# Opening pass of a language-model tower: stacked queries and keys straight from the projection, remainders subtracted on TensorE

## The reference, cut to what matters

```python
left = jnp.einsum('bad,dr->bar', x, W1)         # W1: 128 x 10, "queries"
right = jnp.einsum('rd,bcd->brc', W2, x)        # W2: 10 x 128, "keys"
scores = jnp.einsum('bar,brc->bac', left, right)
attn = jax.nn.softmax(scores / sqrt(512), axis=-1)
out = jnp.einsum('bac,bcd->bad', attn, x)
```

## Time and profile before

| what | us |
| --- | --- |
| median of 3 timed runs | 1693.22 (1692.04 to 1693.26) |
| the profiled execution, its own time | 1697.35 |
| its span, first to last instruction | 1695.5 |
| opening pass, until the second pass's first matmul | 138.9 |
| second pass with the router | 138.9 to about 256 |

### The profile page before, as it was taken

How to read it: one execution, slowest core, us unless ns; L and a number is a source line. 1 busy time by engine, 2 the same in 40 slices (tenths; PEclk the granted TensorE clock), 3 DMA queues, 4 the chain that set the end, 5 groups by cost and what they waited for, 6 DMA issues and landing times. The chain is left out here.

```text
span 1695.5 us, 37358 instructions
## 1 busy us (share of the span) xinstructions
PE 1521.0 (90%) x8662; PEld 660.5 (39%) x8662; DVE 1242.6 (73%) x3454; ACT 1102.5 (65%) x2137; POOL 1018.9 (60%) x1375
## 2 busy tenths in 40 slices
PE   2767975889999999999999999999999999875998
PEld 0215962233333333333333333333333333212665
DVE  4995866478787878878787887878788887353442
ACT  1432770647878777787877878787777878823333
POOL 6841435466685677767567677757767775423443
PEclk9767986879999999999999999999999999957999
DMA  1321117365454565456456546546645643020221
GB/s 41 77 54 31 45 32 108 50 81 72 70 83 67 70 75 84 62 74 81 61 75 77 77 60 83 75 60 81 77 72 65 85 63 55 10 30 29 62 67 56
DMA packets 134645, 109.27 MB, mean 64 GB/s; under 512 B 24128, under 2 KB 127552, under 8 KB 134592
## 3 DMA queue, kind: packets, MB, share of 16 engines
q1 hardware_dynamic: 132544, 104.45, 41.9%
q0 software_dynamic: 2048, 4.20, 1.0%
HBM read 19.26 MB, written 8.39 MB: 16 GB/s over the span
## 5 line engine op out<-in xcount | busy, mean ns | idle before, releaser
L1122 ACT ACTIVATE probs<-psum 128x512 f32<-128x512 f32 (+3 forms) x1536 | 757.9, 550 | 256.2 <-PE psum L1237 247.4
L1022 DVE TENSOR_REDUCE mx_S<-psum 128x1 f32<-128x512 f32 x512 | 324.7, 679 | 50.3 <-PE psum L1217 50.0
L1022 DVE TENSOR_REDUCE mx_C<-psum 128x1 f32<-128x512 f32 x512 | 316.3, 676 | 32.0 <-PE psum L1217 32.0
L1018 DVE CUSTOM_DVE_ANT_0 psum<-psum,causal 128x128 f32<-128x128 f32 (+3 forms) x512 | 241.4, 515 | 95.3 <-PE psum L1217 94.2
L1217 PE MATMUL psum<-ks_S,qs_S 96*128 96x512 bf16 x512 | 197.0, 395 | 17.9 <-DVE mx_S L1022 8.7
L1217 PE MATMUL psum<-ks_C,qs_C 96*128 96x512 bf16 x512 | 199.8, 398 | 12.2 <-DVE mx_C L1022 9.5
L1237 PE MATMUL psum<-qs_C,ks_C 99*128 99x512 bf16 x512 | 188.6, 387 | 3.3 <-ACT probs L1122 2.9
L1237 PE MATMUL psum<-qs_S,ks_S 99*128 99x512 bf16 x512 | 188.0, 384 | 0.2 <-ACT probs L1122 0.2
L903 POOL CAST parts_q<-f_q 128x512 bf16<-128x512 f32 x48 | 29.2, 609 | 251.1 <-ACT f_q L1113 250.6
L1217 PE MATMUL psum<-ks_T,qs_T 96*128 96x128 bf16 (+3 forms) x512 | 157.4, 310 | 5.1 <-DVE mx_T L1018 3.7
L1237 PE MATMUL psum<-qs_T,ks_T 99*128 99x256 bf16 (+3 forms) x512 | 152.3, 302 | 1.8 <-ACT probs L1122 1.7
(11 more groups left out here) (182 smaller groups left out, 2720.1 us busy)
## 6 DMA issues: line engine op xcount, KB each, us to landing
qs_S<-parts_q SPq DMA_DIRECT2D x96, 128.0 KB, 4.4
ks_S<-parts_k SPq DMA_DIRECT2D x96, 128.0 KB, 4.8
qs_T<-parts_q SPq DMA_DIRECT2D x96, 128.0 KB, 4.5
ks_T<-parts_k SPq DMA_DIRECT2D x96, 128.0 KB, 4.6
qs_C<-parts_q SPq DMA_DIRECT2D x96, 128.0 KB, 4.4
ks_C<-parts_k SPq DMA_DIRECT2D x96, 128.0 KB, 4.8
w_in_S<-in_s_in SPq DMA_DIRECT2D x16, 257.0 KB, 2.8
w_in_T<-in_t_in SPq DMA_DIRECT2D x16, 257.0 KB, 2.7
```

The lines of the kernel that those rows point to most:

```text
L1018: nc.vector.tensor_tensor_reduce(tile[:, 0:last_key], tile[:, 0:last_key], causal[:, T - last_key:T], 1.0, NEG, ALU.add, ALU.max, mx[kind] ...
L1022: nc.vector.tensor_reduce(mx[kind][:, n:n + 1], tile, AX_X, ALU.max, negate=True).then_inc(reduced, 1)
L1122: nc.scalar.activation(probs[:, group_place(kind, b, n // 4), n % 4, t0:T], psum[:, LOGITS + ring_place(kind, b, n, RC), t0:T], ACT.Exp, s ...
```

## The change

The projection's weights are widened from 64 to 128 columns on the host: the 10 query columns stand six times in columns 0 to 59 and the 10 key columns six times in 64 to 123. The projection so writes all six groups of queries to partitions 0 to 59 of a PSUM bank and of keys to 64 to 123. The parts are peeled off inside the bank. ACT rounds the whole bank to bf16 (`part[0]`), and PE adds `minus[:, 0, :]` times that to the bank, where `minus` is a diagonal of -1 in those columns whose group wants a later part. The same is done with `part[1]` and `minus[:, 1, :]`. After it each group of the bank holds what its part is a rounding of, and one rounding copy by ACT (queries) and one by DVE (keys) fills 64 partitions of `qsd` and `ksd`. No part passes through SBUF copies by SP any more, and POOL and DVE make none. In the same diff:
- two banks take turns for the projection; lags shrink to 1, 2 and 3 batches; PE and DVE have two pairs of straight code;
- the normalisation moves from DVE to ACT as scale and shift (`shift` is new on DVE);
- `X` is filled by one transfer of SP for each batch instead of an ACT copy;
- POOL starts to gather when the ids are in, and no longer waits for the other six loads;
- the second pass's first logits wait for all reductions, and `negate(1)` is waited for only ahead of the first mix;
- the matmuls of scores and logits contract over 64 and 67 partitions instead of 96 and 99.

The core of the diff:

```diff
-                def stack(pair):
-                    at_least(sp, stacked, 16 * 2 * NPROD * pair)
-                    sp.wait_ge(lr_lo, 2 * pair + 2)
-                    both = bass.ds(2 * pair, 2)
-                    for g in range(NPROD):
-                        sp.dma_start(qsd[HD * g:HD * g + HD, both, :], parts[0:HD, Q_PARTS[g], both, :])\
...
+                def keep(b, odd):
+                    sp.wait_ge(normed1, b + 1)
+                    sp.dma_start(X[:, bass.ds(NB * b, NB), 0:P], xs[:, odd, :, :]).then_inc(x_kept[odd], 16)
...
-                pool.wait_ge(loaded, 16 * LOADS)
+                pool.wait_ge(ids_in, 16)
...
                 nc.vector.memset(X[:, :, P:P + 1], 1.0)
-                nc.vector.memset(ksd[RA:RA + 32, :, :], 1.0)
+                nc.vector.memset(minus[:], 0.0).then_inc(minus_set, 1)
                 dve.wait_ge(consts, 2)
+                dve.wait_ge(minus_set, 1)
+                for k, columns in enumerate(LATER):
+                    for a, e in columns:
+                        last = nc.vector.tensor_scalar(minus[:, k, a:e], ident[:, a:e], -1.0, None, ALU.mult)
+                last.then_inc(minus_set, 1)
+                nc.vector.memset(ksd[RA1:RA1 + 32, :, :], 1.0)
...
# DVE, first_norm(b, odd), after the statistics of batch b
+                    for k in range(2):
+                        if exists(b - SCORE_LAG):
+                            c = b - SCORE_LAG
+                            dve.wait_ge(scored, 2 * c + k + 1)
+                            nc.vector.tensor_reduce(mx[:, bass.ds(NB * c + 2 * k, 2)],
                                                     psum[:, 2 * k:2 * k + 2, :], AX_X, ALU.max).then_inc(reduced, 1)
+                        if k == 0 and exists(b):
+                            dve.wait_ge(std1, b + 1)
...
+                            nc.vector.scalar_tensor_tensor(out=shift[:, odd, :], in0=mv[:, :, 0], scalar=-1.0,
+                                                           in1=rstd[:, odd, :], op0=ALU.mult, op1=ALU.mult)\
+                                .then_inc(shift1, 1)
+                        if k == 0 and exists(b - PART_LAG):
+                            c = b - PART_LAG
+                            dve.wait_ge(taken[1], c + 1)
+                            nc.vector.tensor_copy(ksd[0:RA1, bass.ds(c, 1), :].rearrange("p o t -> p (o t)"),
+                                                  psum[KEYS_AT:P, LR[odd], :]).then_inc(k_ready, 1)
...
# ACT, factors(b, odd), c = b - PART_LAG: in this order
+                        nc.scalar.activation(part[0][:], psum[:, LR[odd], :], ACT.Copy).then_inc(part_ready[0], 1)
+                        nc.scalar.activation(xT[:], psum[:, TURN, :], ACT.Copy).then_inc(xT_ready, 1)
                         nc.scalar.activation(std[:], mv[:, :, 1], ACT.Sqrt, bias=eps_t[:, 0:1]).then_inc(std1, 1)
+                        nc.scalar.activation(part[1][:], psum[:, LR[odd], :], ACT.Copy).then_inc(part_ready[1], 1)
...
+                        for n in range(NB):
+                            last = nc.scalar.activation(xs[:, odd, n, :], tokens(h, b, n), ACT.Identity,
+                                                        bias=shift[:, odd, n:n + 1], scale=rstd[:, odd, n:n + 1])
...
+                        nc.scalar.activation(qsd[0:RA1, bass.ds(c, 1), :].rearrange("p o t -> p (o t)"),
+                                             psum[0:RA1, LR[odd], :], ACT.Copy).then_inc(q_ready, 1)
...
+                def take(c, odd, k):
+                    pe.wait_ge(part_ready[k], c + 1)
+                    nc.tensor.matmul(psum[:, LR[odd], :], minus[:, k, :], part[k][:], start=False, stop=(k == 1),
+                                     skip_group_check=True).then_inc(taken[k], 1)
...
# PE, factors(b, odd), t, c, d = b - 1, b - 2, b - 3: four transposes of t, then
+                        scores(d, 0)
+                        take(c, odd, 0)
+                        nc.tensor.matmul(psum[:, LR[1 - odd], :], w12_t[:], xT[:], start=True, stop=False,
+                                         skip_group_check=True).then_inc(lr_ready, 1)
+                        take(c, odd, 1)
+                        scores(d, 1)
```

More of the change, by code:

```diff
@@ L26 @@
 RB = RA + NPART
+D1 = 10
+KEYS_AT = P // 2
+RA1 = P // 2
+RB1 = RA1 + NPART
 GQ = H // 4
@@ L201, in embed_and_mix @@
         xT = sb("xT", [P, T])
-        parts = sb("parts", [64, NPART, B, T], BF16)
+        part = [sb("part0", [P, T], BF16), sb("part1", [P, T], BF16)]
+        minus = sb("minus", [P, 2, P], BF16)
         qsd = sb("qsd", [P, B, T], BF16)
@@ L269, in _ @@
                 sp.dma_start(norm_cols[:], norms).then_inc(loaded, 16)
-                def stack(pair):
-                    at_least(sp, stacked, 16 * 2 * NPROD * pair)
-                    sp.wait_ge(lr_lo, 2 * pair + 2)
-                    both = bass.ds(2 * pair, 2)
-                    for g in range(NPROD):
-                        sp.dma_start(qsd[HD * g:HD * g + HD, both, :], parts[0:HD, Q_PARTS[g], both, :])\
[L278 to L284, removed]
+                def keep(b, odd):
+                    sp.wait_ge(normed1, b + 1)
+                    sp.dma_start(X[:, bass.ds(NB * b, NB), 0:P], xs[:, odd, :, :]).then_inc(x_kept[odd], 16)
+                halves_of_pairs(sp, keep, 1, B // 2, B // 2)
                 for half in range(2):
@@ L320, in fetch @@
                         ).then_inc(got[b % 2], 16)
[L322 to L331, removed]
+                for b in range(B):
+                    fetch(b)
                 def root(stats, var, done, number, mv, vare, rstd, used=None):
@@ L502, in factors @@
-                    if exists(b):
[L503 to L509, removed]
+                    if exists(c):
+                        act.wait_ge(taken[0], c + 1)
+                        at_least(act, taken[1], c)
+                        nc.scalar.activation(part[1][:], psum[:, LR[odd], :], ACT.Copy).then_inc(part_ready[1], 1)
@@ L558, in turn_maxima, with scores @@
                         .then_inc(max_turned, 1)
+                def scores(c, half):
+                    at_least(pe, reduced, 2 * c - 1 + half)
+                    for n in range(2 * half, 2 * half + 2):
+                        last = nc.tensor.matmul(
+                            psum[:, n, :], qsd[0:RA1, bass.ds(c, 1), P * n:P * n + P].rearrange("p o t -> p (o t)"),
+                            ksd[0:RA1, bass.ds(c, 1), :].rearrange("p o t -> p (o t)"), start=True, stop=True)
+                    last.then_inc(scored, 1)
+                def take(c, odd, k):
+                    pe.wait_ge(part_ready[k], c + 1)
+                    nc.tensor.matmul(psum[:, LR[odd], :], minus[:, k, :], part[k][:], start=False, stop=(k == 1),
+                                     skip_group_check=True).then_inc(taken[k], 1)
                 def factors(b, odd):
@@ L574, in factors @@
-                    if exists(b):
-                        pe.wait_ge(normed1, b + 1)
-                        at_least(pe, xT_ready, b)
-                        for n in range(NB):
-                            last = nc.tensor.transpose(psum[:, TURN, P * n:P * n + P], xs[:, odd, n, :], ident[:])
-                        last.then_inc(turned1, 1)
-                    if exists(b):
-                        pe.wait_ge(xT_ready, b + 1)
-                        at_least(pe, lr_rem, b)
-                        nc.tensor.matmul(psum[0:64, LR, :], w12_t[:], xT[:], start=True, stop=True).then_inc(lr_ready, 1)
@@ L1533, in thirds @@
         return w[0:P], w[P:2 * P], w[2 * P:3 * P]
-    w12 = np.zeros((P, 64), np.float32)
-    w12[:, 0:10] = a["attn_W1"]
-    w12[:, 32:42] = a["attn_W2"].T
+    w12 = np.zeros((P, P), np.float32)
+    for g in range(NPROD):
+        w12[:, D1 * g:D1 * g + D1] = a["attn_W1"]
+        w12[:, KEYS_AT + D1 * g:KEYS_AT + D1 * g + D1] = a["attn_W2"].T
     given = {
```

115 lines of the change are left out of this document (61 added, 54 removed).

## The result

The changed kernel takes **1702.32 us** (median of 18 runs, 1693.04 to 1707.49) against 1692.88 (median of 18, 1691.12 to 1693.76) for the kernel before in the same comparison: ratio 1.0053, 95% interval 1.0042 to 1.0064. That is slower by more than 0.2%. I had predicted 1668.3 and gave "slower" 0.04.

The account below looks back on a forecast made before the run. DVE and POOL were taken to fill the opening pass's steps. Starting the second pass at 114.0 instead of 138.9 saves 24.9 us: 1697.35 becomes 1672.4, less 4.1 gives 1668.3 us; range 1652 to 1682.

Parts of the forecast that it names:

- some other loss: Catch-all without a place or mechanism: an unnamed loss eats the gain; chance 0.04.
- The one about straight code and loops: Opening pass: loops entered at batch 4 cost two more 2.4 us stalls, PE at slower clock; 1680 us; chance 0.15.
- The gather's start: Opening pass on POOL: gather after the ids alone begins about 2.5 us sooner; first statistics near 10.9, 1.2 gained.
- The early idle stretches: Opening pass before batch 4: 10 us of idle stretches stay whole, so batch 4's statistics begin at 40.7.
- The rival in which the gather binds: Opening pass: steps catch up with POOL, first logits at 98 to 104, time 1652 to 1658; chance 0.20.
- The step: Opening pass, per batch from batch 4: 5.85 us at the slower clock, 4.8 at the faster, taken as 5.3.
- half and half: PE's clock in the opening pass: slower and faster level taken in equal parts, giving a 5.3 us step.
- The key copy: DVE's step in the opening pass: copying keys out of PSUM, 64 partitions by 512, taken as 0.65 us.
- The tail: Opening pass from batch 15's statistics to the last reduction: 14.5 us, then 0.5 to the first logits at 114.0.
- SP's maxima rows: End of opening pass: first half's maxima rows land before 114, within a microsecond or two of the first logits.
- Table loads: ACT's step in the opening pass: two 1.28 us loads between root and normalisation; step 8.4, time 1706; chance 0.03.
- the 4.1: Whole kernel: the profiled run lay 4.1 us above the timed median, so 1672.4 became 1668.3.

Follow-up runs that it names:

- experiment 3: The kernel before with 38 idle DVE instructions ahead of the second pass: 1728.92 us, median of three, ratio 1.0213.
- experiment 6: The changed kernel with 90 idle DVE instructions right ahead of the expert loop: 1667.93 us, ratio 0.9855.
- experiment 11: The changed kernel with four pairs of straight DVE code in the opening pass instead of two, no idle instructions: 1663.49 us, ratio 0.9826.
- experiment 7: The changed kernel with 90 idle DVE instructions ahead of the second pass, an earlier file run again on a third chip: 1664.62 us, ratio 0.9831.
- experiment 1: The changed kernel with 90 idle DVE instructions ahead of the second pass, first run: 1723.54 us, ratio 1.0161.
- experiment 2: The changed kernel with 128 idle DVE instructions ahead of the second pass: 1767.75 us, ratio 1.0403.
- experiment 4: The changed kernel with 97 idle instructions on ACT ahead of its expert loop, DVE's code not moved: 1760.61 us, ratio 1.0387.
- experiment 9: The changed kernel with 62 idle DVE instructions ahead of its expert loop: 1667.58 us, timed once.
- experiment 10: The changed kernel with 218 idle DVE instructions ahead of its expert loop: 1681.99 us, timed once.
- experiment 12: The changed kernel with four pairs of straight DVE code, and POOL waiting for all seven loads before gathering: 1667.87 us, ratio 0.9845.
- experiment 5: The changed kernel run again unchanged on another chip: 1697.29 us, ratio 1.0025.
- experiment 8: The changed kernel with 22 idle DVE instructions ahead of its expert loop: 1683.0 us, timed once.

## Why the prediction was wrong

By its own steps:

- **"The second pass behind it keeps its instructions, and so do the later stages. I carry the difference in the start of the second pass to the end without loss."** This is the step that failed. The instructions are the same, but not their places in DVE's stream. 33.75 us were gained up to the second pass and 42.3 us lost in the expert loop. Experiments 3 and 6 show both halves by themselves: the loss without the change, and the change without the loss. My rivals had no case for it; only the 0.04 for "some other loss" covers it, without a mechanism. The one about straight code and loops was weighed for the opening pass's own loops only, and there experiment 11 shows no effect of DVE's.
- The Trainium skill, Runtime: NRT & Kernel Launch, section Instruction fetch mechanics, says that a taken branch to a page outside the fetched window stalls. The runs agree on the stall (3.84 us at the closing branch), and they differ on the size of a block: the fetches of DVE are of 8 KB (0.44 MB in 54), where the page has 16 KiB. Packets of 16 KB are found on q8 alone. I had cited that rule and put it to the wrong loop. The question to ask was which loops lie *behind* the lines that change in number.
- *The gather's start*: the first one at 2.93 (about 3.0 expected), the first statistics at 11.23 (10.9).
- *The early idle stretches* were kept whole, as 10 us, and the changed kernel has none: batch 4 at 29.55 instead of 40.7. This is why the opening pass was better than forecast. The rival in which the gather binds came nearest to its times (batch 15 at 85 to 90, measured 88.48), but for another reason: the last gather was issued at 81.83 and its engine was through 5.7 us before batch 15's statistics began.
- *The step*: 5.36 us, forecast 5.3. Single steps from batch 4 on lie between 4.65 and 7.06, a wider band than the 4.8 to 5.9 given, so the mean is right and its make-up only in part. The clock was 0.83 from 62 to 104 us, not the half and half taken. The key copy took 0.69 (0.65), four scale-and-shifts 1.65 as before, the projection with 128 weight columns 2.08 at the slower clock (1.97 with 64).
- *A reading of the kernel before*: it was put at "about 6.2 a batch until batch 15". Its batches 4 and 15 start at 42.22 and 105.18, which is 5.72 a batch; the first four of these steps take 4.8 on average, and only from 61.53 on do they take 6.1 and more. No term of the sum rests on it.
- *The tail*: 105.17 - 88.48 = 16.7, forecast 14.5 to the last reduction and 0.5 behind it, 1.7 too short. `negate(0)` runs in the midst of the last reductions (DVE's from 98.05 to 99.38), which I had left out.
- Taken together: 114.0 - 11.15 (idle stretches) + 0.6 (steps, 11 x 0.06) + 1.7 (tail) = 105.2.
- *SP's maxima rows* were no bound: their first transfer is issued at 99.47, and the first logits start at 105.17, right behind the turning of the last maxima.
- *Table loads*: none, as forecast.

With the loop in a good place the working's answer comes out: 1668.3 predicted, 1667.93, 1664.62 and 1663.49 measured in experiments 6, 7 and 11. That it comes so close is in part luck, since two errors work against each other in it. The opening pass gained 8.8 us more than forecast, and I took 4.1 us off because the profiled run before lay that far above its median. Without the first error the profiled execution would have been put at 1672.4 - 8.8 = 1663.6. Experiment 11 has 1662.73 for that run and 1663.49 for the median, so the 4.1 were a matter of that one run and not to be carried over. In experiment 6 the 90 idle instructions add up to 3 us.

**What stays open.** Nothing that I ran explains the early idle stretches of the kernel before, or why experiments 1, 2 and 4 had far more of them, and experiment 3, on the same chip, only as many as the kernel before. In all of them hand-overs are recorded long after the instruction's end while POOL gathers. Whether the transfers of the gather, the chip or its load cause that was not tried. Fetches of instructions hardly do: the kernel before has one such packet from 0 to 45 us, between 28 and 29, though idle stretches end at 25.04, 31.36, 36.26 and 39.08, and experiment 1 has one from 28 to 82 us. So ACT's late starts, which the prediction took in part for stalls of taken branches, are not shown to be such. Nor was it shown which of the loops' blocks the five fetches of a turn replace, since the trace gives their time and size only. Nor is it known how many instructions must be left behind the loop: 0 cost and 38 did not, and nothing between was run. In the changed kernel ten turns grew by 37 us together and the eight stretches on "issue" make up 29.9 of them; where the rest lies is open, and so is why its time wanders between 1693 and 1707.

## What to carry to other kernels

A change in the *number* of instructions moves every loop behind it on that engine, and a loop like this one of 312 instructions can change from no fetches to five in every turn. Before you carry a gain to the end, ask for each engine which long hardware loop follows and look for the instruction row in the table of DMA queues. After the change compare that row first: 30 packets against 84 named the cause in one line. Mend the place by the amount of straight code rather than by idle instructions: 90 cost up to 3 us here and 218 some 16.

## What the runs showed of the hardware

- A DVE loop of 312 instructions runs without a fetch in three blocks of 128 with 38, 60 or 66 instructions to spare (the kernel before and experiments 1, 6, 7 and 9 to 12). It fetches five blocks a turn when it ends at a border (the changed kernel and experiments 2 to 5) or lies in four (experiment 8, timed once). That costs 1.9 to 3.7 us in a turn of 74.8.
- The stalls show up in two ways. With the loop's end at a border, "issue" stretches of up to 3.9 us stand at the branch (eight in 800 us, 29.9 us). In experiment 8 there is none, and the 1.9 us a turn are found as longer waits for PE, up to 3.1 us instead of 1.8.
- A hand-over can come up to 21.8 us after the work is done in a stretch where GpSimd issues indirect transfers (experiment 1). Over 54 us of it PE was busy 11.13 us and its clock stood at 0.50, that is 1.2 GHz. In experiment 2 the view gives 1.00 for the same stretch, though four transposes take 1.11 us in both, which is the length of the slower clock in the earlier trace rows (0.66 at the faster). So the clock column of these first stretches is to be held against the length of a matmul. Windows view, experiment 1 and then experiment 2:

```profile
28.00:82.00 54.00, 11.13 (x20) 2.73 (x20) 7.42 (x29) 7.40 (x18) 40.80 (x44) 0.50 0.23 62
28.00:82.00 54.00, 10.86 (x20) 2.60 (x18) 6.75 (x25) 6.71 (x17) 40.80 (x44) 1.00 0.24 62
```
